# Row scatters of two routing stages in groups of four, each group issued after the preceding four have landed

## The reference

```python
x = x + moe_conv(ln_c(x))          # router: 2 of 4 experts (3x3 conv, group norm, silu) + a shared 1x1 conv
t = tokens(x)                      # 16384 tokens of 128 channels
t = t + ffn_top2(ln_t(t))          # 8 experts, hidden 341, silu(h1) * h3, each token goes to 2 of them
x = images(t)
x = x + dynamic_conv(ln_c(x))      # depthwise 3x3, its weights made from the pooled image
t = tokens(x)
t = t + switch_ffn(ln_t(t))        # 8 experts, hidden 512, relu, each token goes to 1, capacity 2560
x = images(t)                      # non-finite values replaced after the last ffn
```

## Time and profile before

| | us |
|---|---|
| time, median of 3 runs | 2088.11 |
| lowest, highest | 2087.66, 2089.25 |
| span of the profiled execution, first to last instruction | 2373.5 |
| own time of the profiled execution | not given beside its span |

### The profile page before, as it was taken

One profiled execution on the slowest core, in us unless ns is written; L12 is line 12 of the kernel. 1 busy time (PEld: TensorE's weight loads), 2 busy tenths in 40 slices (PEclk: granted clock), 3 DMA queues, 4 the chain that ended last, 5 costly groups with the idle time before them and its releaser, 6 DMA issues.

```text
span 2373.5 us, 40208 instructions
## 1 busy us (share of the span) xinstructions
PE 1745.3 (74%) x8924; PEld 941.9 (40%) x8925; DVE 1521.7 (64%) x5423; ACT 1020.1 (43%) x1718; POOL 1040.3 (44%) x1196
## 2 busy tenths in 40 slices
PE   0387777776667775699999999287877868899822
PEld 0333333333333432354445445154544444444312
DVE  1856555545455554577777777476766647788678
ACT  0433333333233332476666667135455524555411
POOL 0003333333333334576566666525455344666600
PEclk9889888878888887799999999599899979999955
DMA  9300001001000002322222221412211013222044
GB/s 267 102 19 28 28 28 36 28 31 33 33 31 28 27 19 59 87 81 74 71 73 79 74 72 46 106 40 60 72 56 45 18 40 95 72 81 72 19 133 151
DMA packets 180085, 149.22 MB, mean 63 GB/s; under 512 B 19302, under 2 KB 161822, under 8 KB 179960
## 3 DMA queue, kind: packets, MB, share of 16 engines
q1 hardware_dynamic: 153336, 98.05, 14.9%
q0 software_dynamic: 26624, 49.93, 6.2%
HBM read 76.00 MB, written 77.34 MB: 65 GB/s over the span
## 4 chain that ended last, share of the span: by engine, by line
PE 38%; DVE 22%; issue 13%; another core or an unknown queue 11%; ACT 7%; POOL 5%; SPq 2%; DMA 1%; ACTq 1%; DVEq 1%; POOLq 0%
PE banks L734 10%; PE banks L736 9%; PE banks L735 9%; PE banks L729 6%; ACT work L1043 3%; POOL slot_rows L618 2%; SPq L429 2%; DVE small L1896 1%; PE banks L747 1%; PE banks L946 1%; DVE small L1392 1%; DVE small L1247 1%; POOL tokens L673 1%; POOL tokens L670 1%
## 5 line engine op out<-in xcount | busy, mean ns | idle before, releaser
L639 POOL DMA_INDIRECT ffn_rows<-work x448 | 471.0, 1051 | 293.9 <-issue 182.1
L618 POOL DMA_INDIRECT slot_rows<-work,small x384 | 387.8, 1010 | 325.5 <-issue 153.3
L729 PE MATMUL banks<-small,work 128*128 128x128 f32 x1472 | 239.9, 308 | 300.8 <-ACT work L1043 118.2
L729 PEld LDWEIGHTS banks<-small,work 128*128 128x128 f32 x1472 | 193.9, 158 | 379.4 <-issue 170.7
L1784 DVE TENSOR_TENSOR work<-work 128x512 f16<-128x512 f32 x376 | 261.4, 695 | 12.8
L734 PE MATMUL banks<-work,wb_h 128*128 128x512 f16 x648 | 247.7, 382 | 26.6 <-DVE work L1800 9.7
L735 PE MATMUL banks<-work,wb_h 128*128 128x512 f16 x648 | 247.0, 381 | 0.0
L736 PE MATMUL banks<-work,wb_l 128*128 128x512 f16 x648 | 246.9, 381 | 0.0
L734 PE MATMUL banks<-work,wa_h 128*128 128x512 f16 x576 | 243.4, 423 | 3.6 <-ACT work L1074 3.3
L735 PE MATMUL banks<-work,wa_h 128*128 128x512 f16 x576 | 243.1, 422 | 0.0
L736 PE MATMUL banks<-work,wa_l 128*128 128x512 f16 x576 | 241.9, 420 | 0.0
(11 more groups left out here) (307 smaller groups left out, 3110.6 us busy)
## 6 DMA issues: line engine op xcount, KB each, us to landing
wa_l<-slot_rows SPq DMA_DIRECT2D x112, 264.0 KB
work<-ffn_rows SPq DMA_DIRECT2D x48, 512.0 KB, 5.2
ffn_rows<-small SPq DMA_DIRECT2D x32, 256.0 KB, 3.7
work<-in_x SPq DMA_DIRECT2D x16, 512.0 KB, 3.3
out_image<-work SPq DMA_DIRECT2D x16, 512.0 KB, 2.6
ffn_rows<-work POOLq DMA_INDIRECT x448
slot_rows<-work,small POOLq DMA_INDIRECT x384
slot_rows<-small SPq DMA_DIRECT2D x17, 264.0 KB, 4.1
```

The costliest lines, as they stand in the source:

```text
L618: pool_e.indirect_dma_start(slots, bass.IndirectOffsetOnAxis(ap=slot_i[:, row_buffer(p, i, k), tt:tt + 1], axis=0), rows[row_buffer(p, i, ...
L639: pool_e.indirect_dma_start(dst, bass.IndirectOffsetOnAxis(ap=idg[old.v][:, qq, 0:1].bitcast(I32), axis=0), yt[old.u][:, qq, :], None, bou ...
L729: last = pe.transpose(dst[:, tt * P:(tt + 1) * P], x, ident)
```

## The change

Before the fifth scatter of each buffer POOL waits until the buffer's first four have landed. In stage A, where a second buffer follows, it also waits before that buffer's first scatter until all eight of the first have landed. An image thus has 3 waits in stage A and 1 in stage C, 64 in all. `landed` is what the buffer's semaphore stands at when all scatters of the images before have landed; `row_buffer` names the buffer of an image and choice; `apart` is a semaphore increment that keeps two waits of one engine from falling on one instruction.

```diff
                 for k in range(choices):
+                    landed = 16 * TPI * (i.b if choices == 2 else i.h)
                     for tt in range(TPI):
+                        if tt == TPI // 2:
+                            pool_e.wait_ge(sem(f"{p}scattered_rows{row_buffer(p, i, k)}"), landed + 16 * tt)
+                            apart(pool_e)
+                        elif k and not tt:
+                            pool_e.wait_ge(sem(f"{p}scattered_rows{row_buffer(p, i, 0)}"), landed + 16 * TPI)
+                            apart(pool_e)
                         pool_e.indirect_dma_start(
```

## The result

| | us |
|---|---|
| changed kernel, median of 4 runs | 2121.74 (2116.97 to 2123.36) |
| before, median of 4 runs | 2088.68 (2087.66 to 2091.82) |
| ratio | 1.0155, 95% interval 1.0142 to 1.0167 |
| forecast | 2129, range 2084 to 2160 |

What follows compares the result with a forecast made beforehand. The chain was a mixture, TensorE 38%, VectorE 22%, with holes assigned to the recorded execution. First buffer 33, second buffer 0, transition 4 and stage C 4 made 41 on 2088.1: 2129 us, range 2084 to 2160, own range 2116 to 2148.

Steps and rivals of the forecast that it cites:

- The holes: Long waits in stages A and C, 261 us of the span, taken to belong to the recorded execution, not timed runs.
- The projected step of 35.8 us: Stage A's step without holes: 34.6 us plus 1.2 for the first-buffer landing behind the row statistics.
- Price of one wait: Each POOL wait: landing 1.43 plus restart 0.90 less gap 0.30, plus 0.2 for a longer scatter: 2.2 us.
- First buffer of stage A: Its wait delays ScalarE's overwriting of the buffer for the next image: 15 x 2.2 = 33 us.
- its rival: In stage A, the row statistics, which release ScalarE's L1043 at 186.22; the landing was put at 187.4.
- The clock: Rival in stage A: longer TensorE rests lower its clock, 22 us more, 2151; chance 0.11.
- Second buffer: Stage A's two further waits, 4.4 us an image, taken as nothing; 8 us if the cover is gone.
- From A to the FFN: Tile 4's load waits for stage A's last landing: 4 us taken, up to 6.6 if not hidden.
- Stage C: One wait an image, between nothing and 20 us depending on the timed step; 4 us taken.
- The gain rival: Holes also in timed runs, and landings every four scatters let held-back signals through: 100 us less, 2029; chance 0.13.
- hidden: Rival: the landing of stage A's first eight scatters is early enough and nothing shows, 2088 to 2092; chance 0.12.
- Half: Rival: scatter pitch 0.97 in timed runs, 20 us in A, nothing in stage C, transition 4: 2112; chance 0.12.

Runs made afterwards that it cites:

- second profile: Kernel before the change, run and profiled again with no edit: 2088.24 us, ratio 0.9996, span 2084.4, no holes.
- the two profiles: Profiles of the changed kernel's first run (2121.74 us) and of the same kernel once more, unedited (2123.07 us, ratio 1.0167).

## Why the prediction was right

- *The holes.* Right: they were of the recorded execution, and the sum had to be made on the step without them. The projected step of 35.8 us was too short, 38.8 measured; each of the two kernels has it, so it is not in the difference.
- *Price of one wait.* 2.2 forecast, 1.9 measured. The landing and the restart were about right (2.03 with 0.30 off); the 0.2 for a long first scatter behind the rest is not there, it takes 0.97. The 1.78 of the first scatter was read wrongly: it does not go with the rest before it, but with an instruction of VectorE (last section).
- *First buffer of stage A.* The term that decided, and mis-sized: 33 forecast, 25.6 measured by the run with it alone. The mechanism is the one forecast. In one step of the unchanged kernel ScalarE's rows (second profile)

```profile
497.75 3.18 ACT L1043 ACTIVATE work<-tokens,small 128x128 f32 x8 [4.02 <-DMA slot_rows<-work,small]
...
537.76 3.19 ACT L1043 ACTIVATE work<-tokens,small 128x128 f32 x8 [3.26 <-DMA slot_rows<-work,small]
```

start 2.4 and 1.5 us behind the row statistics, which VectorE had ready at 495.39 and 536.27; in the changed kernel

```profile
514.24 3.19 ACT L1050 ACTIVATE work<-tokens,small 128x128 f32 x8 [5.89 <-DMA slot_rows<-work,small]
...
557.03 3.19 ACT L1050 ACTIVATE work<-tokens,small 128x128 f32 x8 [4.66 <-DMA slot_rows<-work,small]
```

4.1 and 2.9 us behind theirs (510.10, 554.17). That is +1.8 and +1.4. Over the thirteen steps it is +24.8 us, 1.9 a step, the price of the wait. TensorE's rest has grown by only 20.5, 1.6 a step. Most of the difference hides before ScalarE's next instruction: in the six steps of the unchanged kernel where the landing was not behind the row statistics, that activation waited some 0.6 us for VectorE's scale, 3.7 together, as here

```profile
383.03 1.20 ACT L1074 ACTIVATE work<-banks,small 128x1024 f32<-128x1024 f32 x1 [0.62 <-DVE small L1611]
```

and in no step of the changed kernel does it wait:

```profile
395.24 1.19 ACT L1081 ACTIVATE work<-banks,small 128x1024 f32<-128x1024 f32 x1
```

So the forecast had the price 0.3 too high, and it let all of it show because it had the landing 1.2 us behind its rival in every step; in six of the thirteen it was not behind at all.
- *The clock.* A rival at 22 us, and a part of the truth: TensorE's transposes in the unchanged kernel

```profile
501.08 1.06 PE L729 MATMUL banks<-small,work 128*128 128x128 f32 x8 [2.37 <-ACT work L1043]
```

rested 2.37 us and kept the higher clock (1.06 us for eight of them); in the changed kernel

```profile
517.57 1.94 PE L736 MATMUL banks<-small,work 128*128 128x128 f32 x8 [4.06 <-ACT work L1050]
```

they rested 4.06 and took 1.94 us. Only some steps fall, which cost 7.2 and 3.6 us over thirteen steps in the two profiles; the rival had it in all fifteen.
- *Second buffer.* Taken at nothing; nothing measured. The forecast's cover, POOL's time before L653, was just enough: 1.4 us of it are left in the steps shown, 0.2 to 0.3 in the tightest.
- *From A to the FFN.* 4 forecast for tile 4 waiting on the last landing; 3 to 5 by time, with a rest of 4.1 us in the trace, and only together with the first-buffer wait.
- *Stage C.* 4 forecast, nothing measured. The bound of 19.0 us for the step was too low. POOL in the unchanged kernel (second profile)

```profile
1420.14 0.30 POOL L687 COPY work<-work 128x64 f16<-128x64 f16 x1 [2.53 <-DVE work L2007]
...
1440.83 0.30 POOL L687 COPY work<-work 128x64 f16<-128x64 f16 x1 [2.51 <-DVE work L2007]
```

has a step of 20.7 us and 2.5 to spare, so its own work is 18.2 as forecast; in the changed one

```profile
1436.94 0.29 POOL L694 COPY work<-work 128x64 f16<-128x64 f16 x1 [0.61 <-DVE work L2014]
...
1447.27 0.97 POOL L625 DMA_INDIRECT slot_rows<-work,small  x1 [2.17 <-DMA slot_rows<-work,small]
...
1457.69 0.30 POOL L694 COPY work<-work 128x64 f16<-128x64 f16 x1 [0.67 <-DVE work L2014]
```

the wait takes 2.17 - 0.30 = 1.9 of that and the step is 20.75.
- *The gain rival* fell with the second profile: without holes there is nothing to let through. The *hidden* case holds for 48 of the 64 waits (taken by themselves), not for the 16 that decide. *Half* would have been 2112, 10 us below the result where the forecast is 7 above it. Its terms for stage C and the transition came true, but its reason did not: the gap of 0.30 is there in the runs.

Sum of the parts: 25.6 + 0 + 0 + 3 to 5 = 29 to 31 of 33 to 34. The remaining 2 to 5 us have no place in the traces; they are of the size of the runs' intervals. Without them the forecast's sum would be 11 us too high and not 8, so a part of its closeness is luck. A slip: the 2148 at the upper end of the forecast's own range does not follow from 15 us more, which gives 2144.

## What to carry to other kernels

Here a wait for a landing cost where another engine waits for the landings behind it and has nothing later to wait for; the same wait cost nothing where its engine was idle anyway. So count who else waits, not how many waits there are. Where a profile's span is far above the timed median, profile again before reading holes as a cost. Advancing a path can give back less than delaying it takes: measure how far the next in line is in every step, not in one. Here it was due within a microsecond in all of them.

## What was not expected of the hardware

The span of one and the same kernel was 2373.5 us in one recorded execution and 2084.4 in another. A fall of the granted clock to 0.52 in a single step of stage C cost 5 us (25.8 for 20.8), in a stage that the edit did not touch.

In 15 of the 16 images of the changed kernel scatter 12 takes 1.83 to 1.86 us and not 0.97. The wait is not what makes it long: in the unchanged kernel it is scatter 14, in nine of the images, with 1.18 to 2.03, and the first scatter of nearly every image. The rows of VectorE show what goes with it. Unchanged kernel, second profile, just before the first scatter at 525.14, and changed kernel, just before scatter 12 at 561.62:

```profile
524.77 1.29 DVE L1621 SCALAR_TENSOR_TENSOR work<-work,small 128x1024 f32<-128x1024 f32 x1 [0.52 <-ACT work L1074]
```

```profile
561.34 1.28 DVE L1628 SCALAR_TENSOR_TENSOR work<-work,small 128x1024 f32<-128x1024 f32 x1 [2.58 <-ACT work L1081]
```

From 200 to 830 us of both profiles every scatter that starts while this instruction runs (26 and 29 of them) ends 0.84 to 1.01 us behind its end: 525.14 + 1.78 is 0.86 behind 524.77 + 1.29, and 561.62 + 1.85 is 0.85 behind 561.34 + 1.28. Scatters that start with it or before it take 0.97 or 0.98. No run tests this by an edit, so what joins the two is open.
